# A fused graph-attention kernel: another order of the slots of a step on TensorE

## The reference

```
h = relu(layernorm(x))
q, k, v = h @ Wqs[head], h @ Wks[head], h @ Wvs[head]         # 4096 x 64 each
scores = (q @ k.T) / 8 + 0.01 * eye - 1e16 * (1 - max(adj, eye))
att = softmax(scores, axis=-1)                                # 4096 x 4096
out = x + sum over heads of att @ v @ Wo[head]
```

## Time and profile before

| what | value |
|---|---|
| median of three runs | 2705.91 us |
| profiled execution | 2709.6 us |
| its span | 2708.1 us |
| PE (TensorE) busy | 2630.7 us, 97% |
| DVE (VectorE) busy | 2253.6 us, 83% |
| ACT (ScalarE) busy | 1850.8 us, 68% |
| POOL (GpSimd) busy | 1280.6 us, 47% |
| late moves, SyncE and GpSimd | 2048 issues each |
| DMA moved | 418.51 MB, mean 155 GB/s |

### The profile page before, as it was taken

How to read it: one execution, slowest core, us unless ns; L and a number is a source line. 1 busy time by engine, 2 the same in 40 slices (tenths; PEclk the granted TensorE clock), 3 DMA queues, 4 the chain that set the end, 5 groups by cost and what they waited for, 6 DMA issues and landing times. The chain is left out here.

```text
span 2708.1 us, 58752 instructions
## 1 busy us (share of the span) xinstructions
PE 2630.7 (97%) x17344; PEld 1901.9 (70%) x17344; DVE 2253.6 (83%) x3833; ACT 1850.8 (68%) x3041; POOL 1280.6 (47%) x2418
## 2 busy tenths in 40 slices
PE   7899999999999999999998999999999999999997
PEld 5666777767777776766766777777777777777775
DVE  6788888888888888888847888888888888888885
ACT  3576777767767676776745777777777777777774
POOL 2356655566565556655512444444444444343433
PEclk9999999999999999999999999999999999999999
DMA  6367766677776677776652566656565656555654
GB/s 163 111 143 177 184 163 175 165 168 167 173 190 170 164 177 166 171 171 169 167 142 76 146 158 151 158 142 145 138 151 145 164 146 162 133 146 138 157 144 106
DMA packets 263358, 418.51 MB, mean 155 GB/s; under 512 B 98944, under 2 KB 119936, under 8 KB 259200
## 3 DMA queue, kind: packets, MB, share of 16 engines
q1 hardware_dynamic: 172032, 228.88, 33.0%
q0 software_dynamic: 89088, 184.69, 29.7%
q10 hardware_dynamic: 2176, 4.19, 0.4%
HBM read 136.31 MB, written 46.27 MB: 67 GB/s over the span
## 5 line engine op out<-in xcount | busy, mean ns | idle before, releaser
L307 POOL DMA_DIRECT2D S<-S x2048 | 1007.8, 500 | 1137.1 <-DVE S L723 1089.6
L702 DVE CUSTOM_DVE_ANT_0 S<-psS,B 128x1024 f32<-128x1024 f32 x1024 | 1228.4, 1218 | 268.3 <-PE psS L449 155.1
L589 ACT ACTIVATE S<-S,negm 128x1024 f32<-128x1024 f32 (+1 forms) x768 | 1095.8, 1428 | 88.8 <-DVE negm L709 88.3
L596 ACT ACTIVATE PT<-psT 128x512 f32<-128x512 f32 x1024 | 595.0, 596 | 267.5 <-PE psT L462 248.5
L449 PE MATMUL psS<-K,QH 128*128 128x512 f32 x2048 | 729.2, 437 | 35.7 <-DVE mx L702 31.5
L449 PE MATMUL psS<-K,QL 128*128 128x512 f32 x2048 | 642.5, 395 | 0.0
L462 PEld LDWEIGHTS psT<-ident,S 128*128 128x128 f32 x4096 | 481.2, 140 | 192.0 <-issue 73.5
L462 PE MATMUL psT<-ident,S 128*128 128x128 f32 x4096 | 608.0, 276 | 7.8 <-ACT S L589 4.9
L723 DVE STREAM_TRANSPOSE S<-S 128x2048 f32<-128x2048 f32 x256 | 590.2, 2306 | 27.6 <-PE psO L486 23.7
L472 PE MATMUL psO<-PT,V 128*64 128x256 f32 x4096 | 492.1, 382 | 0.0
L486 PE MATMUL psO<-S,V 128*64 128x256 f32 x4096 | 470.3, 382 | 2.0 <-DMA S<-S 2.0
(11 more groups left out here) (51 smaller groups left out, 967.9 us busy)
## 6 DMA issues: line engine op xcount, KB each, us to landing
S<-S SPq DMA_DIRECT2D x2048, 64.0 KB, 3.1
S<-S POOLq DMA_DIRECT2D x2048, 64.0 KB, 2.9
B<-in_adj POOLq DMA_DIRECT2D x128, 256.0 KB, 7.2
bias_scratch<-B SPq DMA_DIRECT2D x32, 1024.0 KB, 5.8
B<-bias_scratch SPq DMA_DIRECT2D x128, 256.0 KB, 5.1
hq<-hT_scratch SPq DMA_DIRECT2D x32, 256.0 KB, 3.5
RB<-rden_scratch SPq DMA_DIRECT2D x128, 64.0 KB, 3.2
S<-in_x SPq DMA_DIRECT2D x8, 512.0 KB, 3.6
```

Of the source, the lines that this page charges most:

```text
L307: pool.dma_start(dst, src).then_inc(late_sent[q][half], 16)
L589: nc.scalar.activation(part, part, ACT.Exp, bias=negm[:, h % 2, q:q + 1], accum_out=sums[:, h % 2, q, e:e + 1]).then_inc(probs_ready, 1)
L596: nc.scalar.activation(PT[:, s % RING, :], psT[s % 2][:, :], ACT.Copy).then_inc(pt_act, 1)
L702: nc.vector.tensor_tensor_reduce(out=part, in0=psS[j % 2][:, :], in1=B[:, q, k * SLOT:(k + 1) * SLOT], scale=SCALE, scalar=LOWEST, op0=ALU ...
```

## The change

Only the order inside PE's `step` changes. No instruction is added or taken away, and no other engine's program changes. The first score slot of a step now comes ahead of the first transposed slot; transposed slots 0 and 1 stand in a row; after the first values, a score slot again leads; the projection moves from between score slots 0 and 1 to ahead of transposed slot 6; and score slots 0 and 1 alternate with transposed slots 6 and 7.

```diff
-            for s in range(4):
+            def next_scores(j):
+                if nxt:
+                    scores(i1, h1, j)
+
+            next_scores(2)
+            transposes(i, h, 0)
+            transposes(i, h, 1)
+            next_scores(3)
+            if nxt2 and h % 2 == 0:
+                query(i2, h2, h2 == 0, isinstance(i, int) and i == 0 and h == 0)
+            for s in range(2, 4):
                 transposes(i, h, s)
-                if nxt:
-                    scores(i1, h1, 2 + s)
-                if s == 1 and nxt2 and h % 2 == 0:
-                    query(i2, h2, h2 == 0, isinstance(i, int) and i == 0 and h == 0)
+                next_scores(2 + s)
             for s in range(4):
                 values(i, h, s)
             for s in range(4, 6):
+                next_scores(2 + s)
                 transposes(i, h, s)
-                if nxt:
-                    scores(i1, h1, 2 + s)
-            transposes(i, h, 6)
-            transposes(i, h, 7)
-            if nxt2:
-                scores(i2, h2, 0)
             if prev and h % 2 == 0:
                 if nxt2:
                     pe.wait_ge(q_lo, count(i2, h2, 1, 2))
                 project(*last_step(i, h))
-            if nxt2:
-                scores(i2, h2, 1)
+            for s in range(6, TS):
+                transposes(i, h, s)
+                if nxt2:
+                    scores(i2, h2, s - 6)
             values_late(i, h, range(LATE))
             for s in range(4, TS):
                 values(i, h, s)
```

## The result

The changed kernel takes 2716.74 us (median of 11 runs, 2711.72 to 2723.46), where the kernel before took 2705.91 (11 runs, 2698.93 to 2712.35). The ratio is 1.0049, with a 95% interval of 1.0038 to 1.0060: slower by 13 us (10 to 16). The forecast was 2728 us, so the direction is right, and the forecast of 22 us is 1.7 times the loss.

What follows compares the result with a forecast made beforehand. PE, busy 97%, was taken as the bound, with DMA waits behind many first-group mask waits. 10 us of PE's own chain plus 7 + 4 + 1 of the DMA chain made 22 us, so 2728 us; range 2709 to 2746.

Steps and rivals of the forecast that it cites:

- PE's own chain: PE's matmuls in each step: 0.09 us longer in odd, 0.10 in even steps, hidden in 16; 10 us in all.
- y: Time of a score slot behind values on PE, twice a step; taken as 1.03 us, bounds 0.83 and 1.12.
- The rival of a cheap entry into a score slot: Rival on PE: a score slot behind values takes 0.9 us or less; 2699 us; chance 0.09.
- The late start of the moves: In h = 0 steps query tile 0's transpose, and the late moves it starts, come 0.47 us later against PE.
- the terms of 7, 4 and 1 us: PE's added mask waits: 7 us in h = 1 and 4 in h = 3, first group; 1 in the second.
- the worked step: An h = 1 step of the first group, starting at 526.80: PE was to wait 0.46 us more for masks.
- the 4 us: First group, h = 3: late DMAs and a slot asked for earlier cost 0.25 us in each of 16 steps.
- the DMA chain: Late moves landing later, so VectorE's masks and then PE wait longer: 12 us in all.
- The 1 us for the second group: Added mask waits in h = 1 and 3 of the second group, whose DMA waits are 16.7 / 57.0 of the first's.
- A more even pace for VectorE: Rival: VectorE gets more time between score slots 7 and 0, nothing to be seen; about 2707 us; chance 0.09.
- The harder hit of the DMA chain: Rival: 27 us in place of 11 in first-group h = 1 and 3, or y at 1.12; 2744 to 2748 us; chance 0.17.

Runs made afterwards that it cites:

- kernels with few moves: Only 8 of a step's 32 late moves issued: 2648.65 us on the kernel before, 2663.66 us on the changed kernel.
- loads behind the moves: On the kernel before, in h = 2 the second query tile's late moves go ahead of bias and adjacency loads: 2733.11 us, ratio 1.0057.

## Why the prediction was right or wrong

**PE's own chain: right in kind, a little small.** The step that carries the result is that a block costs what its neighbours make it, and that two T in a row and a score slot ahead of late values are paid in each step. The number y, which no row of before shows, was taken as 1.03 from a score slot after a standstill; it is 1.03 and 1.04. Forecast: 0.09 us in an odd step and 0.10 in an even one, hidden in 16 steps, 10 us. Measured: 0.12 in both in the medians, 13 us over 124 steps and 15 in the kernel's time where no wait for a move hides it. The 0.02 to 0.03 us more a step are within what the rounding of some twenty rows to 0.01 us allows, with the 0.01 of the second y; what else may be in them is open.

**The rule of the Trainium skill** on the change of tiling mode ("TensorEngine Tiling (Array Packing)", Key Properties) agrees with the rows in kind: behind values a score slot costs 1.03 or 1.04 us against 1.00 behind a transposed slot, and a transposed slot 0.42 against 0.36, so both pay at the border. The rival of a cheap entry into a score slot is out. Projection-S against query-T (0.67 against 0.87) was a start offset of the rows, as projection-T shows with 0.86.

**The late start of the moves: right up to the queue, wrong behind it.** The transpose starts 0.28 us after the last score slot, as worked out. What failed is "all that lands for the masks of score slots 4 and 5 in the next step lands 0.47 us later", and with it the terms of 7, 4 and 1 us. In the worked step the mask of slot 5 was to start 7.76 us into the step. It is this, in the changed kernel, on VectorE, and the step's first score slot on PE:

```profile
537.52 1.22 DVE L706 CUSTOM_DVE_ANT_0 S<-psS,B 128x1024 f32<-128x1024 f32 x1 [0.34 <-DMA S<-S]
...
539.68 1.21 DVE L706 CUSTOM_DVE_ANT_0 S<-psS,B 128x1024 f32<-128x1024 f32 x1
```

```profile
530.27 0.73 PE L449 MATMUL psS<-K,QH 128*128 128x512 f32 x2
```

7.25 us into the step, against 7.29 before. In the mean of the 16 steps it starts 7.58 us into the step, against 7.64, and the step takes 18.96 us against 18.88, which is no more than PE's own 0.12; the forecast had 0.45 on top. In h = 3 the mean step went from 19.53 to 19.34 us, so the 4 us did not come either. The masks wait for DMAs that in h = 1 stand behind two stores in the queue: without the stores the first eight land 4.6 us earlier after their issue, and the stores did not move against PE. For h = 3, which has no such stores ahead, no run shows why. The row that would have told of h = 1 was in the trace of before: the same 16 issues take 12.80 us there and 10.09 a step earlier. The prediction counted a transfer from what starts it and not from what is ahead of it.

**The sum.** Forecast 10 + 12 = 22 us. Measured 13 (10 to 16). If PE's own chain is the 15 us of the kernels with few moves, the DMA chain is left with -5 to +1. The two errors have opposite signs, 5 us too little and some 14 too much, and that the time lies in the middle of the range owes something to luck. The 1 us for the second group did not follow from the ratio given for it either: 16.7 / 57.0 of 11 us are 3. A share of PE's loss is hidden in the waits of the first group, as it was assumed for h = 2: these waits did not grow, and in the profiles the first group lost 0.04 us a step (20.00 us against 19.96 in the mean of 62 steps) where the second lost 0.08 (19.45 against 19.36). This is one profile of each kernel.

**The rivals.** A cheap entry into a score slot (y below 0.93) is refuted by the rows. A more even pace for VectorE brought nothing: PE's waits for masks in the first group are 23.3 us against 22.7. The harder hit of the DMA chain did not come. The range of 2709 to 2746 us holds the time.

## What to carry to other kernels

On an engine that is 97% busy, reorder on paper first: write the distance from start to start of each block for each pair of neighbours, sum it for both orders, and take a missing pair from a block that started on an idle array. For a transfer ask what stands ahead of it in its queue, and whether the same issues take longer there than elsewhere, before a later trigger is made a later landing. And where one engine already waits for a transfer, a loss elsewhere is partly given back, so test such a loss in a kernel in which that wait is gone: the difference of 15.0 us came out of five runs each, where the full kernels scatter by more than 10. And before a longer wait is priced, look at the granted clock behind it.

## What was not expected of the hardware

- Two stores of 1 MB ahead of 16 small moves of 64 KB stretch their issue on SyncE from 10.1 to 12.4 - 13.2 us; one such store hardly does (10.20 us in the step shown, 10.87 in the mean of 16).
- Most of the kernel's scatter goes with these transfers: with 8 moves of 32 in a step the five runs of each order lie within 2 us, with all 32 the kernel before lies within 17 us (2694.87 to 2712.09, 23 runs) on the same chip.
- Moving 2 MB of stores behind the moves of the next step costs 32 us; moving one half of them a step ahead wins 17.
- With the loads behind the moves, each standstill of PE of 2.1 to 3.9 us in h = 3 went with a granted clock of half for 3.4 us or more, and none of 1.8 us or less did. It is no fixed rule: with the store behind the moves, waits of 2.3 to 2.8 us in h = 2 came with and without it.
